# Linear attention, a routed transformer block and their sum on one core: four output products move behind the last down block

## The reference

```
xn = layernorm(x)
o  = linear attention with decay over 16 heads (chunk by chunk), from q, k, v = xn @ W_qkvu.T
o  = u * (o * rsqrt(mean(o*o) + eps))
attn = o @ W_out.T
sel = the 256 tokens with the highest router score xn @ w_router
h   = rms_norm(sel) * ln1;  q, k, v = h @ wq + bq, ... (rotated);  causal softmax attention, 16 heads
x1  = sel + heads @ wo
h2  = rms_norm(x1) * ln2;  processed = x1 + (silu(h2 @ w_gate) * (h2 @ w_up)) @ w_down
ffn = xn, but for the selected rows: gate * processed + (1 - gate) * sel
result = x + attn + ffn
```

## Time and profile before

| | us |
|---|---|
| median of 3 runs | 479.21 |
| lowest, highest | 478.12, 479.49 |
| the profiled execution's own time | 481.46 |
| its span in the trace | 479.6 |
| TensorE busy in the span | 465.2 |
| scatter (POOL), from issue to landing | 5.0 |

### The profile page before, as it was taken

The page is one execution under the profiler, slowest core; times in us unless marked ns, Lnnn a source line. Parts: engine busy times, 40 slices in busy tenths (PEclk is TensorE's granted clock), DMA queues, the critical chain, the costliest instruction groups (busy, mean ns, idle before and its releaser), DMA issues. The chain is left out here.

```text
span 479.6 us, 11902 instructions
## 1 busy us (share of the span) xinstructions
PE 465.2 (97%) x4839; PEld 422.3 (88%) x4839; DVE 298.8 (62%) x638; ACT 229.5 (48%) x400; POOL 192.2 (40%) x193
## 2 busy tenths in 40 slices
PE   7999999999999999999999998999999999999994
PEld 7988899998998989989899877998888878999993
DVE  6689676887499999755456856767553436230221
ACT  5951243322276779322443436565666446544430
POOL 3240251111120232041367957360470424689862
PEclk9999999999999999999999998999999999999999
DMA  7967675333522111132731689775557822555403
GB/s 227 398 146 123 121 163 85 105 107 110 167 78 68 58 58 55 47 96 65 260 133 46 220 297 326 223 252 176 182 187 274 254 94 88 160 180 186 156 1 44
DMA packets 40951, 72.14 MB, mean 150 GB/s; under 512 B 5872, under 2 KB 7424, under 8 KB 40768
## 3 DMA queue, kind: packets, MB, share of 16 engines
q1 hardware_dynamic: 40352, 70.06, 47.8%
q0 software_dynamic: 544, 1.31, 1.5%
HBM read 54.03 MB, written 17.32 MB: 149 GB/s over the span
## 5 line engine op out<-in xcount | busy, mean ns | idle before, releaser
L1178 POOL TENSOR_TENSOR wlo<-raw,whi 128x512 fp32r<-128x512 f32 x96 | 124.6, 1330 | 88.5 <-ACT whi L564 88.5
L1252 PE MATMUL banks<-HTh,whi 128*128 128x256 f32 x224 | 65.1, 290 | 0.5 <-DVE rope L922 0.4
L1254 PE MATMUL banks<-HTh,wlo 128*128 128x256 f32 x224 | 63.4, 283 | 0.0
L1253 PE MATMUL banks<-HTl,whi 128*128 128x256 f32 x224 | 63.3, 283 | 0.0
L842 DVE TENSOR_TENSOR A<-banks,DEC 128x512 f32<-128x512 f32 x64 | 39.7, 684 | 29.8 <-PE banks L1325 28.3
L1157 POOL TENSOR_TENSOR state_dec<-state,small 128x128 f32<-128x128 f32 x16 | 8.4, 527 | 114.9 <-DVE state L853 114.9
L564 ACT ACTIVATE whi<-raw 128x2048 fp32r<-128x2048 f32 x24 | 45.8, 1908 | 13.2 <-PE banks L1254 7.2
L1252 PEld LDWEIGHTS banks<-HTh,whi 128*128 128x128 f32 x224 | 42.9, 191 | 2.2 <-issue 1.7
L1253 PEld LDWEIGHTS banks<-HTl,whi 128*128 128x128 f32 x224 | 42.9, 192 | 0.3
L1254 PEld LDWEIGHTS banks<-HTh,wlo 128*128 128x128 f32 x224 | 42.9, 191 | 0.0
L1305 PE MATMUL banks<-xTh,WUh 128*128 128x256 f32 x128 | 37.6, 294 | 0.3 <-DVE WUl L787 0.3
(11 more groups left out here) (242 smaller groups left out, 1282.6 us busy)
## 6 DMA issues: line engine op xcount, KB each, us to landing
X<-in_x SPq DMA_DIRECT2D x16, 256.0 KB, 5.8
xn_all<-XN SPq DMA_DIRECT2D x16, 256.0 KB, 6.9
uo_all<-park_h SPq DMA_DIRECT2D x16, 256.0 KB, 2.3
uo_all<-park_l SPq DMA_DIRECT2D x16, 256.0 KB, 3.0
raw<-in_wq SPq DMA_DIRECT2D x4, 1024.0 KB, 6.8
uoh<-uo_all SPq DMA_DIRECT2D x16, 256.0 KB, 3.0
uol<-uo_all SPq DMA_DIRECT2D x16, 256.0 KB, 3.5
XR<-in_x SPq DMA_DIRECT2D x16, 256.0 KB, 3.6
```

Source lines behind the costliest of these rows:

```text
L1178: ins = Q.tensor_tensor(low[:, k, :], raw[b % 3][:, k, :], high[:, k, :].bitcast(f32), ALU.subtract)
L1252: T.matmul(dst, lh, rh, start=first, stop=False)
L1253: T.matmul(dst, lh, rl, start=False, stop=False)
L1254: return T.matmul(dst, ll, rh, start=False, stop=last)
```

## The change

The products 12 to 15 (`last_outs`) are made behind the last down block D3, 9 to 11 (`late_outs`) where 13 to 15 were, and 0 to 8 in the softmax steps 0, 2, 4, 7 and 10 to 14. So the steps 1, 3, 5 and 8 have no product any more.

For the four last tiles the order of the sum is another: their base rows are made early in the MLP stage (ACT) and stored as they are (`store_base`), the scatter adds `delta` to them in HBM, then SP loads the sums back (`load_sums`, waiting for both scatters), DVE adds the product, and SP stores the rows again. The last tile has a buffer of its own (a fourth XR). Product 15 is made in two halves of 256 columns in two banks (`project_out_half`), with a sum and a store for each half. The four products have banks of their own, B[4], B[5], B[0] and B[1] with B[2], outside `bank_jobs`.

In the last chunk (N = 15) PE makes `attend(15)` before the unit in position 2, not behind it. ACT makes `base(0)` and `base(1)` there, and the square, the high part of uo and the gate's exponential come before the mean square of tile 14 and `block_hi(5)`.

```diff
@@ the lists
-        late_outs = (13, 14, 15)
-        out_steps = [0, 1, 2, 3, 4, 5, 7, 8, 10, 11, 12, 13, 14]
+        late_outs, last_outs = (9, 10, 11), (12, 13, 14, 15)
+        out_steps = [0, 2, 4, 7, 10, 11, 12, 13, 14]
...
+            if kind == "out" and n in last_outs:
+                return (B[4], B[5], B[0], B[1])[n - last_outs[0]]
@@ SP
+            def store_base(N):
+                sp.wait_ge(base_ok, N + 1)
+                sp.dma_start(out_t[N], rows_of(N)[:]).then_inc(base_out, 16)
+
+            def load_sums(N):
+                sp.wait_ge(scattered, 16 * NS), sp.wait_ge(base_out, 16 * len(last_outs))
+                sp.dma_start(rows_of(N)[:], out_t[N]).then_inc(sums_in[N], 16)
...
                 if b == block_of["D0"] + 1:
                     for N in late_outs:
                         store(N)
+                    for N in last_outs:
+                        if N < N_TILES - 1:
+                            load_uo(N)
+                        load_x_again(N)
+                if b == block_of["D0"] + 3:
+                    for N in last_outs:
+                        store_base(N)
+            load_uo(N_TILES - 1)
+            for N in last_outs:
+                load_sums(N)
+            for N in last_outs[:-1]:
+                store(N)
+            for half in range(2):
+                N, cols = last_outs[-1], slice(half * GROUP, (half + 1) * GROUP)
+                sp.wait_ge(half_ok, half + 1)
+                sp.dma_start(out_t[N][:, cols], rows_of(N)[:, cols]).then_inc(stored[N % NXR], 16)
@@ ACT, last chunk and steps
-                if N >= N_TILES - CH:
+                if N == N_TILES - 2:
                     mean_square(N - 1)
                 if N == N_TILES - 1:
-                    block_hi(5)
+                    base(0)
+                    base(1)
...
                     S.activation(sq[:], sums, ACT.Square).then_inc(sq_ok, 1)
                     uo_high(N)
+                if N == N_TILES - 1:
+                    act.wait_ge(sel_ok, NS)
+                    S.activation(gate, sel_score, ACT.Exp, scale=-1.0).then_inc(gate_exp, 1)
+                    mean_square(N - 1)
+                    block_hi(5)
...
-                if h in out_at:
+                if out_at.get(h, 0) > 1:
                     base(out_at[h])
...
+                if j == 0:
+                    for N in last_outs:
+                        base(N)
@@ DVE
                 dve.wait_ge(out_ps, N + 1), dve.wait_ge(base_ok, N + 1)
+                if N in last_outs:
+                    dve.wait_ge(sums_in[N], 16)
...
+            for N in last_outs[:-1]:
+                final(N)
+            for half in range(2):
+                N, cols = last_outs[-1], slice(half * GROUP, (half + 1) * GROUP)
+                dve.wait_ge(half_ps, half + 1), dve.wait_ge(sums_in[N], 16), dve.wait_ge(base_ok, N + 1)
+                V.scalar_tensor_tensor(out=rows_of(N)[:, cols], in0=B[1 + half][:, cols], scalar=r_all[:, N:N + 1],
+                                       in1=rows_of(N)[:, cols], op0=ALU.mult, op1=ALU.add).then_inc(half_ok, 1)
@@ POOL, before the scatter
-                        pool.wait_ge(stored[c], 16 * len(range(c, N_TILES, NXR)))
+                        pool.wait_ge(stored[c], 16 * len(range(c, last_outs[0], NXR)))
+                    pool.wait_ge(base_out, 16 * len(last_outs))
@@ PE
+            def project_out_half(N, half):
+                pe.wait_ge(ur_in[N % NUO], 32 * (N // NUO + 1))
+                cols = slice(half * GROUP, (half + 1) * GROUP)
+                for k in range(NK):
+                    ins = split_matmuls(B[1 + half][:, cols], (uoh[N % NUO][:, k, :], uol[N % NUO][:, k, :]),
+                                        (Woh[:, k, cols], Wol[:, k, cols]), k == 0, k == NK - 1)
+                ins.then_inc(half_ps, 1)
...
+                if N == N_TILES - 1:
+                    attend(N)
                 in_position(N, 2)
                 if N >= N_TILES - CH:
                     rms(N - 1)
-                attend(N)
                 if N < N_TILES - 1:
+                    attend(N)
                     new_keys_values(N)
...
+            pe.wait_ge(sg_ok, 8), pe.wait_ge(pt_ok, FH), pe.wait_ge(ot_lo, FH)
+            for N in last_outs[:-1]:
+                project_out(N)
+            for half in range(2):
+                project_out_half(last_outs[-1], half)
```

More of the change, by code:

```diff
@@ L91, in build @@
         tab = at("tab", 140, [P, NS * 2 * FD])
-        XR = [at(f"XR{i}", kb, [P, DM]) for i, kb in enumerate((140, 142, 190))]
+        XR = [at(f"XR{i}", kb, [P, DM]) for i, kb in enumerate((140, 142, 190, 152))]
         HTh, HTl = (at(n, kb, [P, NK, SEL], f32r) for n, kb in (("HTh", 144), ("HTl", 148)))
@@ L278, in build @@
         xa_in, uo_out = (sems(f"{n}_even {n}_odd") for n in ("xa_in", "uo_out"))
-        xr_in, stored, raw_in, ur_in = (sems(f"{n}_0 {n}_1 {n}_2") for n in ("xr_in", "stored", "raw_in", "ur_in"))
+        stored, raw_in, ur_in = (sems(f"{n}_0 {n}_1 {n}_2") for n in ("stored", "raw_in", "ur_in"))
+        xr_in = sems("xr_in_0 xr_in_1 xr_in_2 xr_in_last")
         shead_in, shid_in, wr_in, sbc_in, score_out = sems("shead_in shid_in wr_in sbc_in score_out")
@@ L283, in build @@
         w_raw = dict(zip("VU", sems("w_raw_v w_raw_u")))
-        picked, scattered = sems("picked scattered")
+        picked, scattered, base_out, half_ps, half_ok = sems("picked scattered base_out half_ps half_ok")
+        sums_in = dict(zip(last_outs, sems("sums_in_0 sums_in_1 sums_in_2 sums_in_3")))
         consts, iota_ok, masks_ok, tok_ok, lag_ok = sems("consts iota_ok masks_ok tok_ok lag_ok")
@@ L314, in build, with rows_of, rows_in @@
         down_ps, delta_ok = sems("down_ps delta_ok")
+        def rows_of(N):
+            return XR[N % NXR] if N < N_TILES - 1 else XR[NXR]
+        def rows_in(N):
+            return (xr_in[N % NXR], 16 * (N // NXR + 1)) if N < N_TILES - 1 else (xr_in[NXR], 16)
         def last_use(b):
@@ L483, in _ @@
                         store(N)
+                    for N in last_outs:
[14 more added lines that the diff above has]
+                sp.dma_start(out_t[N][:, cols], rows_of(N)[:, cols]).then_inc(stored[N % NXR], 16)
             for c in range(NXR):
-                sp.wait_ge(stored[c], 16 * len(range(c, N_TILES, NXR)))
+                sp.wait_ge(stored[c], 16 * (len(range(c, N_TILES, NXR)) + (c == last_outs[-1] % NXR)))
         @block.scalar
@@ L586, in uo_high, with base @@
                 S.activation(park_h[:, N % 2], uo[:, N % 2], ACT.Copy).then_inc(uo_hi, 1)
+            def base(N):
+                act.wait_ge(*rows_in(N)), act.wait_ge(gains_ok, 1)
+                S.activation(rows_of(N)[:], rows_of(N)[:], ACT.Identity, scale=gain[:, N:N + 1],
+                             bias=shift[:, N:N + 1]).then_inc(base_ok, 1)
             def in_position(N, position, tiles):
@@ L645, in _ @@
                     block_hi(4)
[L646 to L653, removed]
             def normalised(h):
@@ L944, in final @@
                 dve.wait_ge(out_ps, N + 1), dve.wait_ge(base_ok, N + 1)
+                if N in last_outs:
+                    dve.wait_ge(sums_in[N], 16)
                 dve.wait_ge(r_ok, 1 + N // (N_TILES // 2))
-                V.scalar_tensor_tensor(out=XR[N % NXR][:], in0=job_bank("out", N)[:], scalar=r_all[:, N:N + 1],
-                                       in1=XR[N % NXR][:], op0=ALU.mult, op1=ALU.add).then_inc(final_ok, 1)
+                V.scalar_tensor_tensor(out=rows_of(N)[:], in0=job_bank("out", N)[:], scalar=r_all[:, N:N + 1],
+                                       in1=rows_of(N)[:], op0=ALU.mult, op1=ALU.add).then_inc(final_ok, 1)
             hs_of = (hs, delta)
@@ L1337, in project_out @@
                 pe.wait_ge(o_w_hi, 1), pe.wait_ge(o_w_lo, 1), pe.wait_ge(ur_in[N % NUO], 32 * (N // NUO + 1))
-                bank_free(("out", N))
+                if N not in last_outs:
+                    bank_free(("out", N))
                 for k in range(NK):
@@ L1578, in gate_up @@
                         elif k == "U":
-                            pe.wait_ge(final_ok, N_TILES)
+                            pe.wait_ge(final_ok, last_outs[0])
                         ins = pair(B[first + m % 2], b, p)
```

6 lines of the change are left out of this document (4 added, 2 removed).

## The result

The changed kernel takes 481.38 us in the median of 19 executions, the kernel before 479.42 beside it: ratio 1.0039 [1.0024, 1.0055]. It is slower by 0.4%, where 472.4 was forecast.

What follows compares the result with a forecast made beforehand. TensorE was taken as the bound, busy 465.2 of 479.6 us. Products -11.0, last chunk -3.85, tail +8.0 sum to -6.85 us, so 472.4 us from the median of 479.21; range 471.2 to 477.0.

Steps and rivals of the forecast that it cites:

- part 1: Softmax steps: four products leave the steps and the place behind them, 11.0 us less, with a 0.55 us wait at unit 10.
- Cost taken: nothing: MLP stage: four base rows on ACT, 3.2 us of work, and SP's extra transfers were taken to cost no time.
- Rival (a): Between 300 and 400: PE's slow clock returns with new short waits at units 8 and 10; price 1.65 us, time 474.0, chance 0.14.
- The wait at unit 10: Softmax steps: PE waits 0.55 us for the bank unit 9 used, until DVE's rotation has read it; ends 0 and 2.8.
- The four products: Softmax steps: each product takes 12 matmuls, 2.72 us, with it; four give 11.0 us if something else keeps up with PE.
- The tail of 14.9: After the last down matmul: scatter, loads, sums and stores take 14.9 us in place of 6.95; ends 14.3 and 17.1.
- rival (b): Tail: loads of the sums land slowly behind the scatters' writes; price about 3 to 4 us, time 476, chance 0.13.
- part 3: The new tail behind the last down matmul: two chains, PE's products and the transfers with DVE's sums; grows by 8.0 us.
- The last chunk alone: Last chunk reordered without the product move: wait of 1.75, slow clock 1.65 and 1.0 at unit 8 go, 4.4 us.
- Unit 8: Last chunk: starts at about 286.1 in place of 287.12, 1.0 us earlier, as ACT's last evacuation starts sooner.
- Rival (d): Steps 1, 3, 5, 8: DVE's rotations keep their old length, so 11.0 us don't return; 4.1 slower, 483.3, chance 0.06.
- The move itself: Four products moved behind the last down block: of the 11.0 us that left, 3.0 remain after the tail grows by 8.0.

Runs made afterwards that it cites:

- e1: The change with the four late base rows on ACT, and their stores on SP, one MLP part later; 476.09 us, ratio 0.9925 to before.
- e0: The changed kernel measured again with no edit, for a second profile; 481.28 us, ratio 1.0033 to before.
- g1: The change with eleven extra matmuls that nothing reads, on TensorE ahead of block G2; 479.14 us, ratio 0.9994 to before.
- f4: e1 with product 15 whole: one bank, one sum, one store; 475.41 us, ratio 0.9935 to before.
- f3: The change with SP's stores of tiles 9 to 11 and loads of x ahead of G2's load; 476.19 us, ratio 0.9950 to before.
- e2: The kernel before with only the reordered last chunk, without the move of the four products; 474.90 us, ratio 0.9899 to before.
- h1: e2 measured again, beside b2 on one chip; 474.92 us, ratio 0.9906 to before.
- b2: e1 with the gate's DVE instructions in the second last step, products 0, 1, 2 in steps 0, 3, 5, product 15 whole; 472.84 us, ratio 0.9868.
- e3: The change with the last chunk in the old order, so only the four moved products; 483.79 us, ratio 1.0087 to before.

## Why the prediction was wrong, step by step

**The step that failed** stands in part 1: "Cost taken: nothing", for the four base rows on ACT in the MLP stage. I counted their 3.2 us of work and took "late by an estimated 1 us" for what is queued behind them. I did not count what they wait for: rows of x that SP issues behind three stores and a block, and they met a DMA share of 0.96 in 400 to 420, where I had taken 0.38 (0.44 in 400 to 420 before). ACT is in order, so its 4.8 us of waiting went to the silu and to the high part of G2 as well: that part came 5.4 us late (413.69 for e1's 408.32), not 1, and PE stood 3.07 us. The text had the loads in its list of "extra transfers", but no row of what they would find; the earlier trace rows had one of 7.7 us, which I used for the tail alone. "PE waiting in G2 for a block's low part would show that the base rows on ACT cost something": it did.

**Its second half is the clock.** Behind that wait comes the half clock, 2.5 us (e0 against the first profile; g1). Rival (a) was this mechanism at the wrong place and a smaller price. It is most of the 3.3 us by which the typical execution is slower than the profiled one. The Trainium skill, TensorE: Matmul & The Clock Gate, section "HAM oscillation — how this bites in real kernels", says that a matmul kernel loses its full clock to waits for data between bursts of matmuls; e0 and g1 agree with it at G2, the first profile does not. The length of the wait alone does not decide it here: behind 3.07 us the first profile kept 1.00, behind 1.84 and 1.93 f4 and e1 did, and in before, g1 and f3 the clock fell behind waits of 1.75 to 1.94.

**The wait at unit 10** was forecast at 0.55 and measured 1.64, and one of 0.99 at unit 12 was not forecast: 2.1 us more. My layout took every add of DVE at 0.7 and had no term for the gate. In the changed kernel two adds took 1.07 (290.04) and 1.55 (302.28) and the gate's instruction 1.18, all beside POOL's split. The trace of before had such a row too, an add of the same shape inside POOL's split of 285.57 to 291.03, which takes 0.68 where POOL does not split (282.14 in the change):

```profile
286.99 1.65 DVE L904 TENSOR_TENSOR park_l<-uo,park_h 128x512 fp32r<-128x512 f32 x1
```

A page would have told: the Trainium skill, SBUF — State Buffer, section "Who interferes with whom", says that VectorE and GpSimd share a pair of ports, that a VectorE instruction with two SBUF inputs contends with a GpSimd instruction that reads SBUF, and that one with at most one SBUF input does not, outside the two-port modes, which tensor_scalar can enter. This trace agrees for the adds and for SCALAR_TENSOR_TENSOR on a bank (one input in SBUF), which keeps its length (0.48, and 0.98 a pair) beside POOL. Whether the gate's TENSOR_SCALAR ran in such a mode no run shows; its 1.18 us would fit.

**What held.** The four products were put at 11.0 us and gave 10.2 to 10.4: from unit 8 to T, less the waits and the slow clock, it takes 182.1 us in e2 and h1 and 171.8 to 171.9 in the change, e0 and b2. The tail of 14.9 measured 14.97, with the scatter, the loads and the first sum near their terms (T + 5.7 for 6.05, T + 8.7 as said). That the end fits to 0.1 us is in part luck: in the other runs with halves the tail is 14.7 to 16.8, since the last load from the result takes 3.7 to 5.7 us. This is rival (b)'s mechanism, at up to 1.9 us in place of 3 to 4. The rule of the Trainium skill that part 3 weighs (DMA: Bandwidth & Descriptors, "Anatomy of one DMA") is stated there for transfers that GpSimd issues, and SP issues these; the stores took 1.7 to 2.2 us for a half and 2.1 in the median for a whole. The last chunk alone was forecast at −4.4 and gave −4.5 to −4.7 in the medians (e2, h1). Unit 8 moved 3.4 us, from 287.12 to 283.77, in place of 1.0: the load of K1, which I had as "late next", came sooner too, ACT's high part of it starting at 281.03 where it was 283.57. Step 10 opens at 339.30, some 15 us sooner, as forecast.

**Rival (d)** came nearer to the measured time (483.3) than the forecast did, but mostly for a reason that did not happen. Its sign was there, the two waits for DVE's rotation, but they kept 2.6 of the 11.0 us, where (d) needs at least 6.9, and the steps without a product were otherwise not paced by DVE. Take the cause from the trace, not from the number.

**The sum, corrected**, in profiled executions: −10.2 for the products, −6.7 for the chunk in this execution (the wait of 1.75, 1.6 for the clock, 3.35 at unit 8), +2.6 for the two waits, +3.1 at G2, +8.0 in the tail: −3.2, where the spans say 476.3 − 479.6 = −3.3. An execution like e0 adds 3.0, 2.5 of them for the clock, which leaves −0.3 against the profile of before. That profile was 2.0 us over the median of before; I let it carry over, and of the change the profiled execution is 3.3 under its median. With this −0.3 + 2.0 = +1.7 us, for 1.96 measured. Why before's execution was that long is open. A clock that fell explains at most a part: of the 52 executions of before in the three groups 26 have a mean clock of 0.995 or less, as the profiled one has (0.994), and their median spans are 477.8 to 478.0 by group, against 476.4 to 477.2 for the 24 with 0.997 or more; the profiled span is 479.6.

**The move itself** was forecast at −3.0 (11.0 less 8.0). As written it is +6.4 (e0 less e2, both of group 1). With its three side effects repaired it is −2.1 (b2 less h1), in the profiles 470.5 − 473.4 = −2.9. So the idea's arithmetic was right to within about 1 us, and most of the loss lay in where its helpers were put. How the 8.5 us between the two versions divide among the repairs is measured only for the base rows (e1, 5.2 us); of the rest each alone lies within the noise. b2 also has product 15 whole.

## What to carry to other kernels

When work is taken off the bound engine and its helpers (a load, a base row, a store) are hung on an engine with time to spare, price the wait of each helper for its operands and not its busy time alone, and look at who is queued behind it in order. A wait of the tensor engine can cost nearly twice its length, since its clock may fall behind it (3.1 us and 2.5 more here). A duration is only good for a stretch where the neighbours run as they did where it was read.

## What the runs showed that was not expected

- The clock: after waits of 3.0 to 3.1 us at G2 it stayed at 1.00 in one profiled execution and was 0.57 in 420 to 428 in another of the same kernel; after 1.75 us it was 0.52 for 3.4 us (before), after 1.96 it was 0.57 in 300 to 304 (e3), after 1.81 and 1.94 it was 0.75 to 0.82 in the windows of 296 to 304 (g1, f3), after 1.64, 1.84 and 1.93 it stayed up (the change, f4, e1). Equal waits do not give equal clocks, so one profile can miss several us.
- 2.65 us of useless matmuls made a kernel 2.2 us faster.
- Beside POOL's split a TENSOR_TENSOR of 128x512 took 1.06 to 1.65 us for 0.69, and a TENSOR_SCALAR of 128x2 1.18 for 0.16.
- The stores of 128 KB at the end landed in 1.7 to 2.2 us, those of 256 KB at the same place in 2.0 to 2.7, 2.1 in the median (f4, b2): halving the last store saves next to nothing.
